# A 12-layer state-space block: GpSimd takes its ring products two tiles at a time

## The chip, the cores and the metric

The kernel runs on one core of a Trainium2 chip. TensorE multiplies matrices, VectorE and GpSimd work elementwise, ScalarE evaluates functions, SyncE (SP) issues loads. The metric is the device time of one launch in microseconds (us). A tile here is 128 partitions by 1024 float32 values unless a size is given.

## What is computed

Twelve layers over 8 sequences of 1024 tokens with 256 channels. In each layer the block is

```
xn = layernorm(x);  xp = xn @ pw.T + pb;  z = silu(xp)
for each direction (forward; backward on the reversed sequence):
    u = softplus(xp @ cw.T + cb)
    dt, B, C = split(u @ dbc_w.T)            # 32, 16, 16 columns
    delta = softplus(dt @ dtp_w.T + dtp_b)
    h_t = exp(delta_t * A) * h_(t-1) + (delta_t * u_t) * B_t      # for each of 16 states
    y_t = sum over the states of h_t * C_t  +  D * u_t
x = x + z * (y_forward + y_backward)
```

## The kernel before

The program walks through 96 steps, one per layer and batch element. A step has 64 tiles (`TILES`): 2 halves of the channels, 2 directions, 16 states. Tile k of a step is one recurrence over 1024 tokens for 128 channels. The backward direction's scan runs over the same tile in reverse.

Per tile these things happen, on different engines:

- ScalarE: `tile_exp` writes exp(delta * A) into one of 3 dA tiles (or, for the twelve `SHARED` tiles, into PSUM).
- TensorE: `rep_b` replicates row B of the state to 128 partitions in a PSUM tile `bv`; `add_up` adds the finished product into `y` in PSUM, five tiles behind.
- VectorE: `times_b` multiplies u by B in place (`bv`), `scan` does the recurrence into ring tile k % 8. The order is two `times_b`, then two scans, so tiles are scanned in pairs, and an even tile's scan is the first of its pair.
- GpSimd: `product` multiplies ring tile k % 8 by the replicated row C in `c` tile k % 4, in place. For the `SHARED` tiles, which have their B row loaded by DMA into `v`, GpSimd also does u * B (`times_b` on GpSimd, six tiles ahead).
- SP: `load_c` waits until the product of tile k - 4 is done and loads row C of tile k, broadcast to 128 partitions, 512 KB written per load; `load_b` loads `v`.

Beside this, each step prepares the next step's inputs (layer norm, projections, the softplus of both directions, delta and u). These operations are written into the slots of the 64 tiles by tables of slot numbers (`PROJ_AT`, `XS_AT` and so on): `prepare(k, ...)` issues on each engine what is due in slot k. On GpSimd that is: two normalisations (slots 5, 7, `w<-w,tmp`), two accumulating DMAs for the convolutions' softplus (`XS_AT`, slots 28 and 34), for each direction a subtraction `dbc<-dbc,parts` (`REST_AT` 41, 52) and one `parts<-dbc,parts` (`PARTS_AT` 43, 53), two accumulating DMAs of delta (`DELTA_AT` 43, 54) and the two products u = delta * xs of 128x2048 (`U_AT` 53, 58; the first is direction 1, the second direction 0). `finish`, in slot 5, adds the previous step's z into the output by an accumulating DMA. Each engine works its list strictly in order, so an operation in slot 58 stands behind all products up to 58. The next step's first `times_b` on VectorE waits for both u (`u_ready`).

An engine waits for another through a semaphore: `h_ready` counts finished scans, `p_ready` finished products, `c_loaded` landed C rows, one semaphore for each c tile.

Of the kernel before, what the change touches and what calls it, by code (L numbers as in the profile page):

```python
# [10 lines left out]
P = 128  # L11
# [6 lines left out]
def conv_seq_kernel(nc, x, ln_g, ln_b, proj_w, proj_b, convf_w, convf_b, convb_w, convb_b,  # L18
# [3 lines left out]
    T = HH * WW  # L22
# [7 lines left out]
    TILES = GROUPS * DT  # L30
# [5 lines left out]
    NDA, NR, NC, NV = 3, 8, 4, 2  # L36
# [4 lines left out]
    SHARED = (7, 11, 15, 21, 25, 29, 35, 39, 45, 49, 57, 61)  # L41
# [16 lines left out]
    PROJ_AT, XP_AT = (9, 11, 11, 15), (9, 10, 15, 19)  # L58
    CONV_AT = ((19, 21, 23, 25), (25, 25, 29, 31))
    CONV_OUT_AT = ((19, 23, 24, 24), (27, 27, 30, 30))  # L60
    XS_LOG_AT, XS_AT = ((24, 25), (31, 32)), (28, 34)
    DBC_AT, DBC_OUT_AT = ((32, 36), (41, 43)), ((35, 37), (44, 44))
    DTP_AT, DTP_OUT_AT = ((36, 37, 39, 39), (46, 49, 51, 52)), ((37, 38, 40, 40), (46, 51, 51, 51))
    HI_AT, REST_AT, MID_AT, PARTS_AT = (39, 44), (41, 52), (41, 54), (43, 53)
    DELTA_LOG_AT, DELTA_AT, U_AT = ((40, 40), (52, 55)), (43, 54), (53, 58)
    DIAG_AT, A_STEP_AT = 14, 14
    GATE_AT = 34
    LOADX_AT = 54
# [12 lines left out]
    with ExitStack() as ctx:  # L81
        def sb(name, shape, dt=F32):
            return ctx.enter_context(nc.sbuf_tensor(name, shape, dt))

        def sem(name):
            return ctx.enter_context(nc.semaphore(name))
# [34 lines left out]


        dA = [sb(f"dA{i}", [P, T]) for i in range(NDA)]
        ring = [sb(f"ring{i}", [P, T]) for i in range(NR)]
        c_sb = [sb(f"c{i}", [P, T]) for i in range(NC)]
        v_sb = [sb(f"v{i}", [P, T]) for i in range(NV)]
        assert len(SHARED) % NV == 0


        raw_w = sb("raw_w", [P, DT, D])  # L130
# [68 lines left out]
        h_ready = sem("h_ready")  # L199
        p_ready = sem("p_ready")  # L200
# [4 lines left out]
        c_loaded = [sem(f"c_loaded{i}") for i in range(NC)]  # L205
# [3 lines left out]
        def tiles(it, k):  # L209

            return it * TILES + (SEED + k)
# [32 lines left out]
        def early(it, n):  # L244

            return isinstance(it, int) and it < n
# [107 lines left out]
        def _(pool):  # L354
# [16 lines left out]
            pool.sem_inc(consts_ready, 1)  # L371
            pool.sem_inc(p_ready, SEED)

            def product(it, k, s):
                pool.wait_ge(h_ready, tiles(it, k + 1))
                pool.wait_ge(c_loaded[k % NC], it * (16 * TILES // NC) + (16 * (k // NC) + 16))
                nc.gpsimd.tensor_tensor(ring[k % NR][:], ring[k % NR][:], c_sb[k % NC][:],  # L377
                                        ALU.mult).then_inc(p_ready, 1)

            def times_b(it, k, s):  # L380
                c, d = k // HALF_TILES, (k // NS) % DIRS
                if k == SHARED[0]:
                    pool.wait_ge(u_ready, it * 2 + 2)
                i = SHARED.index(k)
                v = v_sb[i % NV][:]
                pool.wait_ge(vb_loaded[i % NV], it * (16 * len(SHARED) // NV) + 16 * (i // NV + 1))
                nc.gpsimd.tensor_tensor(v, u_of(d, s)[:, c, :], v, ALU.mult).then_inc(vp_ready, 1)  # L387
# [37 lines left out]
            def before_sums(k, n):  # L425

                for j in range(DIRS):
                    if k == XS_AT[j]:
                        pool.wait_ge(ln_done, n * CHAINS + (conv_chain[j] + 1))
                        pool.wait_ge(conv_out, n * (2 * FILLS) + (j + 1) * FILLS)  # L430
                    if k == DELTA_AT[j]:
                        pool.wait_ge(ln_done, n * CHAINS + (delta_chain[j] + 1))
                        pool.wait_ge(dtp_out, n * (2 * FILLS) + (j + 1) * FILLS)
# [8 lines left out]
            def finish(it, s, b):  # L442

                one = out_d[b] if isinstance(b, int) else out_d[bass.ds(b, 1)].rearrange("o p c t -> p (o c) t")
                pool.dma_start(one, z[s][:], accum_op=ALU.add).then_inc(stored, 16)

            def slots(it, s, k0, k1, more, weights, ended=None):
                for k in range(k0, k1):
                    if k == FIRST - 1 and not early(it, 1):
                        pool.wait_ge(gated, (it - 1) * DT + DT)  # L450
                    if more:
                        before_sums(k, it + 1)
                    product(it, k, s)
                    if k + V_AHEAD in SHARED:
                        times_b(it, k + V_AHEAD, s)
                    if k == FIRST - 1 and not early(it, 1):
                        finish(it - 1, 1 - s, ended)
                    if more:
                        prepare(k, it + 1, 1 - s)
                    if more > 1:  # L460
                        prepare(k - TILES, it + 2, s)
# [6 lines left out]
            def begin():  # L468
                pool.wait_ge(primed, 16 * NB)

            run_layers(nothing, slots, first_prepare, begin, tail, nothing, pool)


# [459 lines left out]
```

## Time and profile before

| | |
|---|---|
| median of 3 runs | 20557.72 us (20556.65 to 20569.37) |
| span of the profiled execution | 20567.5 us |
| VectorE, GpSimd, TensorE, ScalarE busy | 96%, 95%, 89%, 57% |
| granted TensorE clock | 0.9 or more of full speed in all 40 slices |
| DMA | 218 GB/s on the mean |
| products on GpSimd | 6144 of 128x1024 |
| a step on the mean, span / 96 | 214.2 us |

The span starts with the first and ends with the last instruction. Idle time of an engine counts only where something else waits for it; the views used below are the page's busy shares, the list of who waited for whom, and the timelines of two engines over the same stretch.

### The profile page before, as it was taken

How to read it: one execution, taken by the hardware profiler on the slowest of the kernel's cores; microseconds unless marked ns; L12 is line 12 of the kernel's file. 1: busy time of each engine (PE TensorE's matmuls, PEld its weight loads, DVE VectorE, ACT ScalarE, POOL GpSimd, SP SyncE). 2: the span in 40 equal slices, each digit the busy share in tenths (PEclk: the TensorE clock that was granted, in tenths of full speed). 3: DMA queues.
4: the chain of work that ended last, by engine and by line, in shares of the span. 5: the costliest groups of instructions: out<-in, count | busy, mean ns of one | idle time of the engine just before them, and what ended most of it. 6: DMA issues, size and time to landing. Idle time of an engine off the chain costs nothing.

```text
span 20567.5 us, 191522 instructions
## 1 busy us (share of the span) xinstructions
PE 18224.6 (89%) x45600; PEld 7539.9 (37%) x45600; DVE 19673.9 (96%) x11520; ACT 11649.3 (57%) x12409; POOL 19457.2 (95%) x8562
## 2 busy tenths in 40 slices
PE   8898888889888888888988888888888888889898
PEld 3333333333333333333333333333333333333333
DVE  7999999999999999999999999999999999999999
ACT  5555555555555555555655555555555555556554
POOL 7999999999999999999999999999999999999999
PEclk9999999999999999999999999999999999999999
DMA  6666666666666666666666666666666666667666
GB/s 203 217 220 217 222 220 217 220 219 223 218 218 223 215 221 218 218 220 218 222 217 222 220 218 223 215 219 217 218 222 216 222 219 219 218 220 223 217 220 202
DMA packets 1212383, 4489.98 MB, mean 218 GB/s; under 512 B 159872, under 2 KB 170624, under 8 KB 1161856
## 3 DMA queue, kind: packets, MB, share of 16 engines
q1 hardware_dynamic: 1078912, 3934.73, 54.7%
q0 software_dynamic: 81408, 503.35, 12.5%
q10 hardware_dynamic: 50688, 36.88, 0.9%
q8 instruction: 459, 7.52, 0.1%
q14 instruction: 916, 7.50, 0.1%
HBM read 3945.94 MB, written 134.22 MB: 198 GB/s over the span
## 4 chain that ended last, share of the span: by engine, by line
PE 33%; issue 28%; DVE 22%; ACT 7%; POOL 6%; DMA 3%; DVEq 1%; ACTq 0%; POOLq 0%; SPq 0%
PE y L719 19%; DVE ring L866 15%; DVE bv L850 6%; PE bank L738 6%; PE bv L709 5%; POOL ring L377 3%; DMA c<-c_rows 2%; ACT pre L555 2%; POOL u L422 1%; ACT bv L547 1%; PE y L731 1%; PE bank L785 1%; ACT dA L547 1%; ACT pre L559 1%; ACT tmp L555 1%
## 5 line engine op out<-in xcount | busy, mean ns | idle before, releaser
L377 POOL TENSOR_TENSOR ring<-ring,c 128x1024 f32<-128x1024 f32 x6144 | 14683.2, 2538 | 803.2 <-DVE ring L866 671.6
L719 PE MATMUL y<-ring,ident 128*128 128x512 f32 x24576 | 11737.2, 605 | 143.1 <-DVE z L872 140.5
L866 DVE TENSOR_TENSOR_SCAN ring<-dA,bv 128x1024 f32<-128x1024 f32 x4992 | 11192.3, 2274 | 192.0 <-ACT dA L547 39.5
L547 ACT ACTIVATE dA<-delta,a_step 128x1024 f32<-128x1024 f32 x4992 | 5608.6, 1143 | 3391.4 <-DVE ring L866 3126.0
L719 PEld LDWEIGHTS y<-ring,ident 128*128 128x128 f32 x24576 | 4745.5, 193 | 4506.3 <-issue 3663.7
L850 DVE TENSOR_TENSOR bv<-u,bv 128x1024 f32<-128x1024 f32 x4992 | 5924.3, 1214 | 437.7 <-PE bv L709 333.9
L709 PE MATMUL bv<-parts,select 128*128 128x512 bf16 x9984 | 3037.4, 386 | 2103.3 <-DVE ring L866 2081.3
L387 POOL TENSOR_TENSOR v<-u,v 128x1024 f32<-128x1024 f32 x1152 | 2907.2, 2524 | 0.0
L547 ACT ACTIVATE bv<-delta,a_step 128x1024 f32<-128x1024 f32 x1152 | 1286.4, 1117 | 2777.4 <-DVE ring L866 2777.3
L709 PEld LDWEIGHTS bv<-parts,select 128*128 128x128 bf16 x9984 | 671.2, 98 | 5707.1 <-DVE ring L866 5104.3
L866 DVE TENSOR_TENSOR_SCAN ring<-bv,v 128x1024 f32<-128x1024 f32 x1152 | 2608.5, 2264 | 2.3 <-POOL v L387 2.3
L738 PE MATMUL bank<-z,wt 128*128 128x512 f32 x3072 | 1413.5, 593 | 3.6 <-ACT xf L552 2.8
L551 ACT ACTIVATE tmp<-bank,vec 128x512 f32<-128x512 f32 x768 | 523.2, 681 | 889.7 <-PE bank L785 508.8
L551 ACT ACTIVATE pre<-bank,vec 128x512 f32<-128x512 f32 x768 | 522.6, 681 | 702.3 <-PE bank L738 658.1
L738 PEld LDWEIGHTS bank<-z,wt 128*128 128x128 f32 x3072 | 583.7, 190 | 740.5 <-issue 665.3
L785 PE MATMUL bank<-dbc,wt_dbc 128*128 128x512 f32 x1536 | 800.0, 614 | 8.4 <-ACT dbc L599 7.8
L738 PE MATMUL bank<-w,wt 128*128 128x512 f32 x1536 | 720.6, 602 | 46.1 <-POOL w L395 44.7
L738 PE MATMUL bank<-pre,mean_w 128*128 128x512 f32 x1536 | 714.6, 598 | 11.7 <-DMA pre<-in_x_dram 11.3
L395 POOL TENSOR_TENSOR w<-w,tmp 128x1024 f32<-128x1024 f32 x192 | 519.1, 2704 | 160.6 <-ACT tmp L649 160.6
L573 ACT ACTIVATE z<-bank,pbias 128x512 f32<-128x512 f32 x384 | 259.8, 677 | 595.0 <-PE bank L738 310.2
L552 ACT ACTIVATE delta<-bank,vec 128x512 f32<-128x512 f32 x768 | 522.3, 680 | 0.0
L404 POOL TENSOR_TENSOR dbc<-dbc,parts 96x1024 f32<-96x1024 f32 x192 | 409.7, 2134 | 76.4 <-PE bank L785 68.5
(66 smaller groups left out, 8904.8 us busy)
## 6 DMA issues: line engine op xcount, KB each, us to landing
c<-c_rows SPq DMA_DIRECT2D x6144, 512.0 KB, 4.6
v<-c_rows SPq DMA_DIRECT2D x1152, 512.0 KB, 5.0
w<-pre POOLq DMA_DIRECT2D x96, 1024.0 KB, 12.2
xf<-tmp POOLq DMA_DIRECT2D x96, 1024.0 KB, 10.9
delta<-pre POOLq DMA_DIRECT2D x96, 1024.0 KB, 8.4
delta<-tmp POOLq DMA_DIRECT2D x96, 1024.0 KB, 10.1
out_dram<-z POOLq DMA_DIRECT2D x96, 1024.0 KB, 13.2
pre<-out_dram SPq DMA_DIRECT2D x88, 1024.0 KB, 7.0
```

The costliest lines, as they stand in the source:

```text
L377: nc.gpsimd.tensor_tensor(ring[k % NR][:], ring[k % NR][:], c_sb[k % NC][:], ALU.mult).then_inc(p_ready, 1)
L387: nc.gpsimd.tensor_tensor(v, u_of(d, s)[:, c, :], v, ALU.mult).then_inc(vp_ready, 1)
L547: nc.scalar.activation(to[:], delta_of(d, s)[:, c, :], ACT.Exp, scale=a_step[s][:, c, n:n + 1]).then_inc(da_ready, 1)
L551: nc.scalar.activation(scratch[j][:, e, half(h)], bank[i % 2][:], ACT.Abs, bias=bias).then_inc(abs_done, 1)
L552: nc.scalar.activation(to[:, e, half(h)], bank[i % 2][:], ACT.Relu, bias=bias).then_inc(done, 1)
L555: nc.scalar.activation(scratch[j][:], scratch[j][:], ACT.Exp, scale=-1.0).then_inc(exp_done, 1)
L709: mm = pe.matmul(bv[k % 2][:, half(h)], select[:, n:n + 1].to_broadcast([P, P]), parts_of(d, s)[:, half(h)], start=True, stop=True)
L719: mm = pe.matmul(y[:, half(h)], ident[:], ring[k % NR][:, half(h)], start=(k % HALF_TILES == 0), stop=(k % HALF_TILES == HALF_TILES - 1), ...
L738: mm = pe.matmul(dst[:], lhs(c), rhs[:, c, half(h)], start=(c == 0), stop=(c == DT - 1))
L785: pe.matmul(bank[i % 2][:], wt_dbc[:, DT + e, :], dbc[:, half(h)], start=True, stop=True).then_inc(dtp_ready, 1)
L850: nc.vector.tensor_tensor(bv[k % 2][:], u_of(d, s)[:, c, :], bv[k % 2][:], ALU.mult).then_inc(v_ready, 1)
L866: nc.vector.tensor_tensor_scan(h, a, b, 0.0, ALU.mult, ALU.add).then_inc(h_ready, 1)
```

## The change

Ring and c tiles become slices of two tensors, `rings` (128 x 8 x 1024) and `c_rep` (128 x 4 x 1024), so that tiles k and k + 1 lie side by side. In each odd slot GpSimd multiplies the pair (k - 1, k) in one instruction of 128x2048. It waits for both scans and for both C rows, and raises `p_ready` by 2 when it is done. In even slots there is no product, and what else stands in an even slot follows directly on the slot before. Loads are issued as before, tile by tile, but since `p_ready` now moves in twos, the loads of a pair become due at the same moment. Three accumulating DMAs move by one slot: XS from (28, 34) to (27, 33), the second of delta from 54 to 55; the second u moves from slot 58 to 59.

```
-    XS_LOG_AT, XS_AT = ((24, 25), (31, 32)), (28, 34)
+    XS_LOG_AT, XS_AT = ((24, 25), (31, 32)), (27, 33)
-    DELTA_LOG_AT, DELTA_AT, U_AT = ((40, 40), (52, 55)), (43, 54), (53, 58)
+    DELTA_LOG_AT, DELTA_AT, U_AT = ((40, 40), (52, 55)), (43, 55), (53, 59)
...
-        ring = [sb(f"ring{i}", [P, T]) for i in range(NR)]
-        c_sb = [sb(f"c{i}", [P, T]) for i in range(NC)]
+        rings = sb("ring", [P, NR, T])
+        ring = [rings[:, i, :] for i in range(NR)]
+        c_rep = sb("c", [P, NC, T])
+        c_sb = [c_rep[:, i, :] for i in range(NC)]
...
-            def product(it, k, s):
-                pool.wait_ge(h_ready, tiles(it, k + 1))
-                pool.wait_ge(c_loaded[k % NC], it * (16 * TILES // NC) + (16 * (k // NC) + 16))
-                nc.gpsimd.tensor_tensor(ring[k % NR][:], ring[k % NR][:], c_sb[k % NC][:],
-                                        ALU.mult).then_inc(p_ready, 1)
+            def products(it, k, s):
+                pool.wait_ge(h_ready, tiles(it, k + 2))
+                for t in (k, k + 1):
+                    pool.wait_ge(c_loaded[t % NC], it * (16 * TILES // NC) + (16 * (t // NC) + 16))
+                two = rings[:, k % NR:k % NR + 2, :]
+                nc.gpsimd.tensor_tensor(two, two, c_rep[:, k % NC:k % NC + 2, :], ALU.mult).then_inc(p_ready, 2)
...
-                    product(it, k, s)
+                    if k % 2:
+                        products(it, k - 1, s)
```

Two places of GpSimd's order in a step. The first is around tiles 51 to 53: `v` is the multiply for tile 57 in slot 51, `dbc0` the rest, `u1_1` the u of direction 1. Before:

```order
L387 TENSOR_TENSOR v0<-u1_0,v0 128x1024
L375 REGISTER_ALU
L376 REGISTER_ALU
L377 TENSOR_TENSOR ring4<-ring4,c0 128x1024
L402 REGISTER_ALU
L404 TENSOR_TENSOR dbc<-dbc,parts0 96x1024
L375 REGISTER_ALU
L377 TENSOR_TENSOR ring5<-ring5,c1 128x1024
L416 ISA
L422 TENSOR_TENSOR u1_1<-delta1_1,w1 128x2048
```

After:

```order
L390 TENSOR_TENSOR v0<-u1_0,v0 128x1024
L405 REGISTER_ALU
L407 TENSOR_TENSOR dbc<-dbc,parts0 96x1024
L377 REGISTER_ALU
L379 REGISTER_ALU
L381 TENSOR_TENSOR ring<-ring,c 128x2048
L419 ISA
L425 TENSOR_TENSOR u1_1<-delta1_1,w1 128x2048
```

The rest now comes ahead of the product of tile 52, which it followed.

The second place is GpSimd from slot 55 to the u of direction 0 (`u0`). Before, it stands behind the product of tile 58 (ring tile 2), and the DMA of delta was issued ahead of these rows:

```order
L377 TENSOR_TENSOR ring7<-ring7,c3 128x1024
L387 TENSOR_TENSOR v1<-u1_0,v1 128x1024
L375 REGISTER_ALU
L376 REGISTER_ALU
L377 TENSOR_TENSOR ring0<-ring0,c0 128x1024
L375 REGISTER_ALU
L377 TENSOR_TENSOR ring1<-ring1,c1 128x1024
L375 REGISTER_ALU
L377 TENSOR_TENSOR ring2<-ring2,c2 128x1024
L420 ISA
L421 ISA
L422 TENSOR_TENSOR u0<-delta0,xf1 128x2048
```

After:

```order
L381 TENSOR_TENSOR ring<-ring,c 128x2048
L390 TENSOR_TENSOR v1<-u1_0,v1 128x1024
L417 DMA delta0<-tmp 128x2048
L377 REGISTER_ALU
L379 REGISTER_ALU
L381 TENSOR_TENSOR ring<-ring,c 128x2048
L377 REGISTER_ALU
L381 TENSOR_TENSOR ring<-ring,c 128x2048
L423 ISA
L424 ISA
L425 TENSOR_TENSOR u0<-delta0,xf1 128x2048
```

`u0` now stands behind the product of tile 59 too, and the DMA of delta behind the product of tile 55 and the multiply for tile 61.

## Rows read from the trace of the kernel before

**Rows 1.** The page: the span, and each engine's busy time (share), instructions.

```profile
span 20567.5 us, 191522 instructions
...
PE 18224.6 (89%) x45600; PEld 7539.9 (37%) x45600; DVE 19673.9 (96%) x11520; ACT 11649.3 (57%) x12409; POOL 19457.2 (95%) x8562
```

**Rows 2.** Waits, whole span: who waited for whom: us, times, longest.

```profile
POOL ring L377 <- DVE ring L866: 671.6, 394, 4.7
...
DVE bv L850 <- PE bv L709: 333.9, 445, 2.6
ACT z L573 <- DMA out_dram<-z: 284.9, 59, 6.1
...
DVE bv L850 <- POOL u L422: 12.9, 1, 12.9
```

**Rows 3.** VectorE's timeline, 11558 to 11656: start, us, line, operation, count, [idle before].

```profile
11560.69 4.46 DVE L866 TENSOR_TENSOR_SCAN ring<-dA,bv 128x1024 f32<-128x1024 f32 x2
...
11594.69 2.26 DVE L866 TENSOR_TENSOR_SCAN ring<-bv,v 128x1024 f32<-128x1024 f32 x1
...
11604.60 2.35 DVE L850 TENSOR_TENSOR bv<-u,bv 128x1024 f32<-128x1024 f32 x2
...
11647.40 4.46 DVE L866 TENSOR_TENSOR_SCAN ring<-dA,bv 128x1024 f32<-128x1024 f32 x2
```

**Rows 4.** GpSimd's timeline, 11563 to 11606, the same step.

```profile
11563.05 4.69 POOL L377 TENSOR_TENSOR ring<-ring,c 128x1024 f32<-128x1024 f32 x2 [0.18 <-DVE ring L866]
11567.68 2.36 POOL L387 TENSOR_TENSOR v<-u,v 128x1024 f32<-128x1024 f32 x1
11569.98 2.37 POOL L377 TENSOR_TENSOR ring<-ring,c 128x1024 f32<-128x1024 f32 x1
11573.04 2.13 POOL L404 TENSOR_TENSOR dbc<-dbc,parts 96x1024 f32<-96x1024 f32 x1 [0.69 <-PE bank L785]
11575.13 2.37 POOL L377 TENSOR_TENSOR ring<-ring,c 128x1024 f32<-128x1024 f32 x1
11577.45 4.54 POOL L422 TENSOR_TENSOR u<-delta,w 128x2048 f32<-128x2048 f32 x1
11581.97 2.12 POOL L409 TENSOR_TENSOR parts<-dbc,parts 32x1024 bf16<-32x1024 f32 x1
11584.07 2.36 POOL L377 TENSOR_TENSOR ring<-ring,c 128x1024 f32<-128x1024 f32 x1
11586.38 0.87 POOL L414 DMA_DIRECT2D delta<-tmp  x1
11586.99 2.65 POOL L377 TENSOR_TENSOR ring<-ring,c 128x1024 f32<-128x1024 f32 x1
11589.30 2.65 POOL L387 TENSOR_TENSOR v<-u,v 128x1024 f32<-128x1024 f32 x1
11591.61 7.28 POOL L377 TENSOR_TENSOR ring<-ring,c 128x1024 f32<-128x1024 f32 x3
11598.57 4.79 POOL L422 TENSOR_TENSOR u<-delta,xf 128x2048 f32<-128x2048 f32 x1
11603.05 4.94 POOL L377 TENSOR_TENSOR ring<-ring,c 128x1024 f32<-128x1024 f32 x2
```

**Rows 5.** The page's DMA issues: count, KB each, median us from issue to landing.

```profile
c<-c_rows SPq DMA_DIRECT2D x6144, 512.0 KB, 4.6
...
delta<-tmp POOLq DMA_DIRECT2D x96, 1024.0 KB, 10.1
```

**Rows 6.** Tile c, landings of two loads: from 8485.3 and 8485.8; from 11550.7 and 11553.0.

```profile
DMA to landing us min/median/max: 4.9/5.3/5.7
...
DMA to landing us min/median/max: 6.4/6.9/7.4
```

**Rows 7.** ScalarE's timeline, 11636 to 11656, the head of the next step.

```profile
11646.97 0.69 ACT L573 ACTIVATE z<-bank,pbias 128x512 f32<-128x512 f32 x1 [5.20 <-DMA out_dram<-z]
11647.56 1.14 ACT L547 ACTIVATE dA<-delta,a_step 128x1024 f32<-128x1024 f32 x1
```

More of the change, by code:

```diff
@@ L123, in conv_seq_kernel @@
         dA = [sb(f"dA{i}", [P, T]) for i in range(NDA)]
-        ring = [sb(f"ring{i}", [P, T]) for i in range(NR)]
-        c_sb = [sb(f"c{i}", [P, T]) for i in range(NC)]
+        rings = sb("ring", [P, NR, T])
+        ring = [rings[:, i, :] for i in range(NR)]
+        c_rep = sb("c", [P, NC, T])
+        c_sb = [c_rep[:, i, :] for i in range(NC)]
         v_sb = [sb(f"v{i}", [P, T]) for i in range(NV)]
-        assert len(SHARED) % NV == 0
+        assert len(SHARED) % NV == 0 and NR % 2 == 0 and NC % 2 == 0
         raw_w = sb("raw_w", [P, DT, D])
```

## The prediction

> **What bounds the kernel now.** I read the busy shares first. VectorE is busy 96% of the span, GpSimd 95%, TensorE 89% [rows 1]: an instruction saved on either of the first two could count, so the question is which of them waits for the other. The waits say it [rows 2]. GpSimd sat 671.6 us before its ring products because the scan on VectorE was not done, in 394 places. The other way round hardly anything stands: VectorE waited for GpSimd's u once (12.9 us), and its largest wait is for TensorE's replicated B rows, 333.9 us. So VectorE sets the pace, and GpSimd follows with some room. There are 96 steps, one per layer and batch element, of 20567.5 / 96 = 214.2 us on the mean; VectorE is idle (20567.5 - 19673.9) / 96 = 9.3 of them, GpSimd 11.6.
>
> The next reading is where GpSimd's room is smallest, since it also makes things VectorE needs at a fixed place. I took one usual step and set both engines' timelines side by side. Tile 51's scan ends at 11565.15 (two scans from 11560.69, 4.46 together) [rows 3]. Product 50 starts on GpSimd at 11563.05, as soon as scan 50 is done, and product 51 right behind it [rows 4]: here GpSimd waits for VectorE (0.18 us idle, released by the scan). From there to the end of the step GpSimd has more to do than VectorE: v for tile 57, one rest, u for direction 1, one parts, one DMA issue, v for tile 61, and then u for direction 0, which starts at 11598.57, takes 4.79 and ends at 11603.36 [rows 4]. The next step's first multiply by B on VectorE needs that u. It starts at 11604.60 [rows 3]. **The room is 1.24 us.** It was like that in nearly every step, since that wait is booked only once in 96 [rows 2]. This is the place on which the forecast rests: whatever makes u later by more than 1.24 us moves the whole of VectorE, once a step.
>
> **What the change removes.** 64 products of 128x1024 become 32 of 128x2048. What one costs is the distance from one start to the next: three products and the step into u take 11598.57 - 11591.61 = 6.96, so 2.32 each. The same engine already runs a two-input multiply of 128x2048, u: 11577.45 to 11581.97 is 4.52, 11598.57 to 11603.05 is 4.48 [rows 4]. I take 4.50 for a pair against 4.64, so 0.14 us less, 32 times a step: 4.5 us of GpSimd work a step. A row's own duration (2.36 for one) overlaps the next start and is not used for this. Most of this is room, not time, since GpSimd is not what is waited for; only the pairs between scan 51 and u are on the path. [...]
>
> **What it adds, one: the grain.** A pair starts when the second scan is done, not the first. Where GpSimd follows VectorE closely, product 50 started at 11563.05; the pair (50, 51) can start at 11565.2 at the earliest. And in the order after, u for direction 0 stands behind pair (58, 59) where it stood behind product 58; the DMA of delta also stands behind pair (54, 55) and v for 61, where it stood behind product 54.
>
> **The path from scan 51 to u, step by step**, with the durations of [rows 4]: pair (50, 51) from 11565.2, 4.50, to 11569.7. v for 57, 2.30, to 11572.0. The rest must wait for TensorE as before, until 11573.04 (the 0.69 idle before it), so 1.04 us of the delay is swallowed there; 2.09, to 11575.13. Pair (52, 53) to 11579.63. u of direction 1, 4.52, to 11584.15. parts, 2.10, to 11586.25. Pair (54, 55) to 11590.75. v for 61, 2.31, to 11593.06, whose recorded end is 11593.4; scan 61, which reads it, starts at 11594.69 [rows 3], so this is still in time. DMA issue 0.61, to 11593.67. Pairs (56, 57) and (58, 59) to 11602.67. u 4.79, to **11607.46**. That is 4.10 us later than 11603.36; less the room of 1.24, VectorE starts its next step **2.86 us later**.
>
> Two small things come on top. The accumulating transfer of delta, issued at 11593.06, takes 10.1 us to land [rows 5], so to 11603.2, and u cannot start at 11602.67: 0.5. And pair (50, 51) may be late itself, because of the loads below, by some 1.4; 1.04 of that is swallowed by the wait at the rest: 0.4. Together 3.75.
>
> **What it adds, two: the C loads.** There are four c tiles. A load was issued when the product four tiles back was done, with three products (6.9 us) to land in. Now the two loads of a pair go out together when the pair two back is done, and have one pair, 4.50 us, plus whatever small work lies between. A lone load lands after 4.6 [rows 5]. Of loads issued behind one another the last is later: two of them 0.48 us apart behind a v load landed after 4.9 and 5.7 [rows 6], so the second 6.2 after the first was issued; without the v load I take 5.5 (0.45 + 5.05, an estimate between the lone load's 4.6 and that 5.7). Where nothing lies between two pairs, that is a wait of 1.0 us. Six of the 32 places are so bare (in front of the pairs that begin at tiles 0, 14, 28, 38, 48 and 50; at 28 only a DMA issue lies between), the others have a v multiply or more (2.3 us) and are covered. Where an accumulating transfer runs beside them loads took 6.4 to 7.4 [rows 6], so in front of pair (48, 49), behind the first delta transfer, I expect 2 to 3 us. Between tiles 26 and 50 these waits cost GpSimd only room: it waits for scans there anyway. In front of u, pairs (52, 53) to (58, 59) have 7 us or more to land in, so nothing is on the path but the 0.4 above. [...]
>
> **What it adds, three: the head of a step.** Behind u, four products (9.3) become two pairs (9.0), but VectorE starts right after u instead of 1.24 later, and pair (0, 1) waits 1.0 for its loads. So against VectorE GpSimd is 1.2 + 1.0 - 0.3 = 1.9, later 1.6 us behind where it was. What hangs on it: the output transfer, for whose landing ScalarE waits 5.20 us before it writes z at 11646.97 [rows 7]. The exp of tile 13 stands behind that, 11647.56 to 11648.70; scan 13 is the second of the two from 11647.40, so about 11649.6 [rows 3]: room 0.9. A delay of 1.6 leaves 0.7 of stall, in the steps that have the wait (59 of 96 [rows 2]), so 0.4 a step. TensorE's sums read the products five tiles later; they are hardly ever waited for, and I charge nothing.
>
> **The sum.** 3.75 + 0.4 = 4.1 us a step on VectorE's chain, at 95 boundaries: 390 us. The profiled span is 20567.5 [rows 1] and the median 20557.7, so the difference is applied to the median: **20950 us**, 1.9% slower. XS issued one slot earlier (27, 33) goes out about as early as before against VectorE; it costs nothing.
>
> **Rivals.** (1) *GpSimd paces, and its saving is what counts*: then 32 x 0.14 = 4.5 us a step off, less the waits for C of bare places in the stretch where it is behind (2 x 1.0), so 2.5 x 96 = 240 us: 20320. It decides if the waits of VectorE for TensorE (333.9) were at bottom waits for a product. Against it: GpSimd waited for scans, 671.6. (2) *No change*: u is not later by more than its room. It needs 2.9 us that I do not see, for instance pairs that take 4.1 instead of 4.50; and the rest of the program the same. 20520 to 20600. (3) *The C loads reach the path to u*. Pair (58, 59) has v for 61, the DMA issue and one pair before it, 2.31 + 0.61 + 4.50 = 7.4 us for its two loads, and the delta transfer starts among them. If loads there land as beside the other transfer, 7.4, plus 0.45 for the later issue and 0.8 for standing behind the first (5.7 - 4.9) [rows 6], the second is there after 8.7, so 1.3 late; and the same in front of (48, 49) and (50, 51) lets the chain start 3 us late instead of 1.4, 1.5 more. That is 2.8 a step on top of 4.1, 95 x 6.9 = 655 us: 21210. It decides from landings of 7.4 us in front of (58, 59). The other bare places do not reach VectorE as long as GpSimd's sum, 202.7 - 4.5 of work and some 5 to 12 of waits for loads, stays under the step. (4) That the pair would be split back into two instructions is ruled out by the compiled order.
>
> **How the numbers follow.** The forecast (u late, 2.9 to 5 us a step, 20780 to 21050) 0.70; the C loads, 21100 to 21350, 0.17; faster 0.08; no change 0.05. A measurement of this kernel tells 0.2% (41 us) from nothing. Slower holds 0.87. The range reaches from the forecast's bottom, 95 x 2.86 = 272 us with some room below it, to the middle of rival 3: 20780 to 21260; some 0.2 is left out.
>
> **What would show it.** Right: u on VectorE's list of waits (its multiply by B waiting for GpSimd's u, some 3.5 us, in nearly all steps); GpSimd's product group near 4.5 us each, 3072 of them; more idle time of GpSimd for c landings, in front of pairs 0, 14 and 48 above all, and less for scans; ScalarE's wait for the output transfer longer. Wrong: if that wait for u stays single, or VectorE's new idle time stands before scans, or before multiplies released by TensorE that itself waited for products, the grain acted elsewhere. If c landings are waited for in front of (58, 59), rival 3 has it.

## The result

The changed kernel takes 21365.07 us (median of 4 runs, 21349.62 to 21379.4) against 20557.63 us: the ratio is 1.0389, 95% interval 1.0377 to 1.0402. Slower was forecast and came, but twice as much of it: 8.4 us a step instead of 4.1, and the time lies outside the range. The profiled execution spans 21347.5 us, 780 us more than before.

The page of the changed kernel, first the span and busy times as in [rows 1], then the two groups of GpSimd and VectorE that carry the change: line, engine, operation, shapes, count | busy, mean ns | idle before, releaser.

```profile
span 21347.5 us, 185442 instructions
...
PE 18395.0 (86%) x45600; PEld 7562.9 (35%) x45600; DVE 19697.5 (92%) x11520; ACT 11641.0 (55%) x12409; POOL 19048.5 (89%) x5490
...
L381 POOL TENSOR_TENSOR ring<-ring,c 128x2048 f32<-128x2048 f32 x3072 | 14090.0, 4632 | 2044.9 <-DMA c<-c_rows 956.8
...
L870 DVE TENSOR_TENSOR_SCAN ring<-bv,v 128x1024 f32<-128x1024 f32 x1152 | 2611.5, 2267 | 359.8 <-ACT bv L551 351.2
```

GpSimd has 409 us less to do and VectorE's work is nearly unchanged (19697.5 against 19673.9, 24 us more), so 756 of the 780 us are idle time of VectorE, and the question is what it waits for. Its list of waits, to be held against [rows 2]:

```profile
DVE bv L854 <- PE bv L713: 368.3, 439, 5.5
DVE ring L870 <- ACT bv L551: 351.2, 93, 5.6
DVE bv L854 <- POOL u L425: 350.1, 96, 12.3
DVE z L876 <- PE y L723: 153.8, 192, 8.5
DVE bv L854 <- issue: 125.0, 34, 5.6
```

Two rows have grown from next to nothing, and both now come once in nearly every step. The wait for u is the one that the prediction rests on: 12.9 us, once, has become 350.1 us, 96 times. The other stands before the scan of a tile whose exp ScalarE writes into `bv`, 351.2 us in 93 places; the prediction does not know it. Together they are 688 of the 780 us more.

**The wait for u.** GpSimd's timeline and then VectorE's at the end of a step (scan 51 ends here at 12018.65), to be held against [rows 3, 4].

```profile
12016.46 9.03 POOL L381 TENSOR_TENSOR ring<-ring,c 128x2048 f32<-128x2048 f32 x2 [2.68 <-DMA c<-c_rows]
12025.44 2.35 POOL L390 TENSOR_TENSOR v<-u,v 128x1024 f32<-128x1024 f32 x1
12027.76 2.12 POOL L407 TENSOR_TENSOR dbc<-dbc,parts 96x1024 f32<-96x1024 f32 x1
12029.85 4.54 POOL L381 TENSOR_TENSOR ring<-ring,c 128x2048 f32<-128x2048 f32 x1
12034.35 4.55 POOL L425 TENSOR_TENSOR u<-delta,w 128x2048 f32<-128x2048 f32 x1
...
12057.35 4.70 POOL L425 TENSOR_TENSOR u<-delta,xf 128x2048 f32<-128x2048 f32 x1
```

```profile
12057.36 1.20 DVE L884 TENSOR_TENSOR w<-pre,bank 128x1024 f32<-128x1024 f32 x1
12062.18 2.36 DVE L854 TENSOR_TENSOR bv<-u,bv 128x1024 f32<-128x1024 f32 x2 [3.62 <-POOL u L425]
```

Pairs (48, 49) and (50, 51) follow each other from 12016.46, so (50, 51) starts about 12020.97, 2.3 us behind scan 51. u ends at 12062.05 (12057.35 + 4.70), 43.4 us behind the end of scan 51; before it was 38.2 (11603.36 - 11565.15), so 5.2 more. VectorE waits 3.62 us.

**The wait at scan 45.** ScalarE's timeline of the changed kernel around it, then VectorE's.

```profile
11988.14 1.13 ACT L551 ACTIVATE dA<-delta,a_step 128x1024 f32<-128x1024 f32 x1
11995.12 1.04 ACT L624 CAST parts<-dbc 64x1024 bf16<-64x1024 f32 x1 [5.84 <-POOL dbc L407]
11996.07 1.11 ACT L551 ACTIVATE bv<-delta,a_step 128x1024 f32<-128x1024 f32 x1
```

```profile
11991.05 2.29 DVE L870 TENSOR_TENSOR_SCAN ring<-dA,bv 128x1024 f32<-128x1024 f32 x1
11997.30 2.29 DVE L870 TENSOR_TENSOR_SCAN ring<-bv,v 128x1024 f32<-128x1024 f32 x1 [3.96 <-ACT bv L551]
```

The exp of tile 45 stands on ScalarE behind a cast, and the cast waits 5.84 us for GpSimd's rest (the subtraction `dbc<-dbc,parts` in slot 41). Before, the same three pieces stood like this (ScalarE, before; the rest started on GpSimd at 11536.35):

```profile
11538.46 1.13 ACT L547 ACTIVATE dA<-delta,a_step 128x1024 f32<-128x1024 f32 x1
11539.50 1.03 ACT L620 CAST parts<-dbc 64x1024 bf16<-64x1024 f32 x1
11540.44 1.11 ACT L547 ACTIVATE bv<-delta,a_step 128x1024 f32<-128x1024 f32 x1
```

No wait at all. Taken from the scan of tile 44 (11541.37 before, 11991.05 after), the rest has gone from 5.0 us ahead of it to 1.9 us behind it. Why it is 6.9 us late is in GpSimd's timeline of the changed kernel, tiles 26 to 41:

```profile
11940.30 4.55 POOL L381 TENSOR_TENSOR ring<-ring,c 128x2048 f32<-128x2048 f32 x1 [4.65 <-ACT pre L563]
11944.77 0.90 POOL L415 DMA_DIRECT2D w<-pre  x1
...
11954.19 4.55 POOL L381 TENSOR_TENSOR ring<-ring,c 128x2048 f32<-128x2048 f32 x1 [1.66 <-DMA c<-c_rows]
11961.88 4.54 POOL L381 TENSOR_TENSOR ring<-ring,c 128x2048 f32<-128x2048 f32 x1 [3.13 <-ACT tmp L563]
...
11968.67 0.85 POOL L415 DMA_DIRECT2D xf<-tmp  x1
...
11981.65 4.54 POOL L381 TENSOR_TENSOR ring<-ring,c 128x2048 f32<-128x2048 f32 x1 [3.05 <-DMA c<-c_rows]
...
11992.94 2.14 POOL L407 TENSOR_TENSOR dbc<-dbc,parts 96x1024 f32<-96x1024 f32 x1
```

Pair (26, 27) is held 4.65 us and pair (32, 33) 3.13 us, by ScalarE's Ln (the logarithm of the softplus): in an odd slot the wait that belongs to the accumulating transfer (`before_sums`) is written ahead of the pair, and since the slots moved from 28 and 34 to 27 and 33 it holds the pair up. The second transfer then goes out at 11968.67, 10.5 us behind the start of scan 34, where it was 6.0 before, and runs beside the C loads for (38, 39). These were issued from 11974.1, 6.1 and 7.0 us to landing, and the pair stands 3.05 us for them:

```profile
L308 SPq DMA_DIRECT2D c<-c_rows x2: 320/680/1040, 11974.1 to 11974.5; - x2
...
DMA to landing us min/median/max: 6.1/6.5/7.0
```

### The profile page after: what moved, and what is told of

Same layout as the page of the kernel before. It is cut to its first block, busy times and chain, and to the rows that moved or that the text cites. A ratio compares the mean times of both kernels' runs of the same rounds, so it can differ in the third digit from the quotient of the medians.

```text
span 21347.5 us, 185442 instructions
## 1 busy us (share of the span) xinstructions
PE 18395.0 (86%) x45600; PEld 7562.9 (35%) x45600; DVE 19697.5 (92%) x11520; ACT 11641.0 (55%) x12409; POOL 19048.5 (89%) x5490
## 4 chain that ended last, share of the span: by engine, by line
issue 25%; PE 21%; POOL 20%; DMA 14%; DVE 14%; ACT 4%; SPq 1%; DVEq 1%; POOLq 0%; ACTq 0%
DMA c<-c_rows 14%; POOL ring L381 14%; PE y L723 12%; DVE ring L870 10%; PE bank L742 5%; DVE bv L854 4%; PE bv L713 3%; POOL u L425 2%; POOL dbc L407 1%; POOL v L390 1%; POOL parts L412 1%; ACT pre L563 1%; ACT pre L559 1%; PE y L735 1%; SPq L308 1%
## 5 line engine op out<-in xcount | busy, mean ns | idle before, releaser
L381 POOL TENSOR_TENSOR ring<-ring,c 128x2048 f32<-128x2048 f32 x3072 | 14090.0, 4632 | 2044.9 <-DMA c<-c_rows 956.8
L723 PE MATMUL y<-ring,ident 128*128 128x512 f32 x24576 | 11864.0, 610 | 331.2 <-POOL ring L381 188.4
L854 DVE TENSOR_TENSOR bv<-u,bv 128x1024 f32<-128x1024 f32 x4992 | 5932.3, 1214 | 859.1 <-PE bv L713 368.3
L713 PE MATMUL bv<-parts,select 128*128 128x512 bf16 x9984 | 3108.4, 394 | 2528.0 <-DVE ring L870 2507.6
L870 DVE TENSOR_TENSOR_SCAN ring<-bv,v 128x1024 f32<-128x1024 f32 x1152 | 2611.5, 2267 | 359.8 <-ACT bv L551 351.2
L390 POOL TENSOR_TENSOR v<-u,v 128x1024 f32<-128x1024 f32 x1152 | 2771.5, 2406 | 0.0
L624 ACT CAST parts<-dbc 64x1024 bf16<-64x1024 f32 x192 | 199.0, 1037 | 535.2 <-POOL dbc L407 535.2
```

Of the source, the lines that this page charges most:

```text
L381: nc.gpsimd.tensor_tensor(two, two, c_rep[:, k % NC:k % NC + 2, :], ALU.mult).then_inc(p_ready, 2)
L713: mm = pe.matmul(bv[k % 2][:, half(h)], select[:, n:n + 1].to_broadcast([P, P]), parts_of(d, s)[:, half(h)], start=True, stop=True)
L723: mm = pe.matmul(y[:, half(h)], ident[:], ring[k % NR][:, half(h)], start=(k % HALF_TILES == 0), stop=(k % HALF_TILES == HALF_TILES - 1), ...
L854: nc.vector.tensor_tensor(bv[k % 2][:], u_of(d, s)[:, c, :], bv[k % 2][:], ALU.mult).then_inc(v_ready, 1)
L870: nc.vector.tensor_tensor_scan(h, a, b, 0.0, ALU.mult, ALU.add).then_inc(h_ready, 1)
```

## The experiments

There were three theories. **A**: two waits of VectorE a step make the loss, for u and at scan 45, fed by the grain of two and by the slots. **B**: the C landings pace everything. **C**: the moved slots alone do it. In the code below, "..." marks lines left out. Ratios are to the kernel before, measured in the same rounds.

**The slots alone.** The kernel before with only the new slot numbers.

```
-    XS_LOG_AT, XS_AT = ((24, 25), (31, 32)), (28, 34)
+    XS_LOG_AT, XS_AT = ((24, 25), (31, 32)), (27, 33)
...
-    DELTA_LOG_AT, DELTA_AT, U_AT = ((40, 40), (52, 55)), (43, 54), (53, 58)
+    DELTA_LOG_AT, DELTA_AT, U_AT = ((40, 40), (52, 55)), (43, 55), (53, 59)
```

> The kernel before with single products, but with the new slot numbers (XS 27 and 33, second DELTA 55, second U 59). Theory A (two waits of VectorE a step make the whole loss: for u at the head of a step, and at scan 45 for ScalarE's exp, which stands behind a cast that waits for GpSimd's rest; both fed by the grain of pairs): the slots alone cost u one product, 2.3 us less the room of 1.24, so about 1.1 us a step and no wait at scan 45, since GpSimd still has its idle 4 us in front of tile 38 to absorb the waits for the Ln: 20660, ratio 1.005. Theory B (waits for C landings set the time): nothing, 1.000. Theory C (the slot moves do it, because GpSimd waits for ScalarE's Ln ahead of tiles 27 and 33): most of the loss, 1.02 or more, with the wait at scan 45 in its waits.

Measured 20842.88 us, ratio 1.0135 (1.0118 to 1.0152). VectorE's waits:

```profile
DVE bv L850 <- PE bv L709: 365.4, 468, 2.4
DVE z L872 <- PE y L719: 257.8, 192, 7.9
DVE bv L850 <- POOL u L422: 163.8, 94, 12.8
...
DVE ring L866 <- ACT bv L547: 1.7, 6, 0.5
```

The wait for u is there (163.8 us; without the 12.8 that the first step has in the kernel before too, 1.6 a step, expected 1.1) and nothing at scan 45, as A says: GpSimd waits 390.3 and 241.9 us for the Ln, and its waits for scans fall by about as much, from 671.6 to 33.7, so single products absorb it. But the loss is more than twice the 0.5% that I expected. The rest is mostly in the second row: z waits 257.8 us. Before:

```profile
DVE z L872 <- PE y L719: 158.9, 192, 7.9
```

This wait is not a later product 63: it ends 49.5 us behind scan 51 in a step of either kernel, since u has only changed places with product 59. z waits for TensorE's last sums, and these are slower. In one step each, the four matmuls ahead of z at the head of a step are

```profile
11624.01 1.88 PE L719 MATMUL y<-ring,ident 128*128 128x512 f32 x4
```

```profile
11791.41 3.51 PE L719 MATMUL y<-ring,ident 128*128 128x512 f32 x4
```

The first row is of the kernel before, the second of this run. The granted clock is 1.00 over the first and 0.53 over the second, which is nearly all at the lower of TensorE's two levels, 1.2 of 2.4 GHz. z waits 0.31 us there and 2.01 here. Over the whole trace these last sums ran at a granted clock under 0.75 at the head of 68 of 96 steps, against 8 before, and z's wait at the head is 137.6 us, against 47.4. TensorE had waited 3.30 us for a scan at 11775.47, and the clock over its next 3.4 us of sums was 0.50; but a wait of 2.12 us stands just ahead of the last sums in both kernels. So what brings the clock down there is not shown; that the late u does it, by holding up the scans that TensorE waits for, was not tested. C falls: the slots alone are 1.35% of 3.9%.

**The grain without the long instruction.**

```
-two = rings[:, k % NR:k % NR + 2, :]
-nc.gpsimd.tensor_tensor(two, two, c_rep[:, k % NC:k % NC + 2, :], ALU.mult).then_inc(p_ready, 2)
+nc.gpsimd.tensor_tensor(ring[k % NR], ring[k % NR], c_sb[k % NC], ALU.mult)
+nc.gpsimd.tensor_tensor(ring[k % NR + 1], ring[k % NR + 1], c_sb[k % NC + 1], ALU.mult).then_inc(p_ready, 2)
```

> The changed kernel with the same waits, the same signals by twos and the same slots, but two instructions of 128x1024 instead of one of 128x2048. Theory A: the loss is the grain's and the slots', not the instruction's; two take 4.64 instead of 4.50, five pairs stand on the way to u and about three on the way to the rest, so 1.1 us a step more than the changed kernel: 21470, ratio to before 1.044. If the long instruction itself did harm, it would come out faster than the changed kernel, under 21300.

Measured 21491.75 us, ratio 1.0455 (1.0437 to 1.0472), as A forecast. Against two short instructions the long one is a gain of 127 us, 1.3 a step, where it stands on the way to what VectorE waits for. The loss is not the instruction's: it comes with the waits and signals of the pair, and with the slots, which are the changed ones here too.

**XS behind the pair.** A 128x1 multiply carries the wait in the even slot.

```
-    XS_LOG_AT, XS_AT = ((24, 25), (31, 32)), (27, 33)
+    XS_LOG_AT, XS_AT = ((24, 25), (31, 32)), (28, 34)
...
+elif more and k in (*XS_AT, *DELTA_AT):
+    q = (*XS_AT, *DELTA_AT).index(k)
+    one = mark[:, q:q + 1]
+    nc.gpsimd.tensor_tensor(one, one, one, ALU.mult)
```

> The changed kernel with XS back in slots 28 and 34, where GpSimd has no product: the wait for ScalarE's Ln and the accumulating transfer then stand behind pairs (26, 27) and (32, 33), not around them (a 128x1 multiply of GpSimd carries the wait). Theory A and C: GpSimd's 4.2 and 2.4 us of waiting for the Ln run beside the pairs, the second transfer goes out some 5 us earlier, the loads of (38, 39) land before they are needed, the rest is early enough and the wait at scan 45 (3.6 us a step) goes; the wait for u (3.4) stays: 21365 - 96 x 3.6 = 21020, ratio 1.022. Theory B: under 1 us a step, 1.035 or more.

Measured 20958.87 us, ratio 1.0194 (1.0177 to 1.0211). Half of the loss is gone, and with it the wait at scan 45; the one for u stays. VectorE's waits (the row for ScalarE's `bv` has 4.5 us left):

```profile
DVE bv L858 <- PE bv L717: 374.9, 448, 7.2
DVE bv L858 <- POOL u L425: 308.3, 96, 12.4
DVE z L880 <- PE y L727: 175.2, 192, 8.5
```

**u early, XS as changed.** Second DELTA back to 54, second u back to 58, where it stands behind pair (56, 57); the same 128x1 multiply.

```
-    DELTA_LOG_AT, DELTA_AT, U_AT = ((40, 40), (52, 55)), (43, 55), (53, 59)
+    DELTA_LOG_AT, DELTA_AT, U_AT = ((40, 40), (52, 55)), (43, 54), (53, 58)
```

> The changed kernel (XS stays at 27 and 33) with only the second DELTA back in slot 54 and the second u in 58, so u stands behind pair (56, 57). Theory A: the wait for u (3.4 us a step) goes, the one at scan 45 (3.6) stays, and with e4 and e5 the two parts add up: 21365 - 96 x 3.3 = 21050, ratio 1.024. If the two waits hide each other, it stays above 1.032.

Measured 21099.48 us, ratio 1.0255 (1.0238 to 1.0272). The mirror image: u is back at one wait, scan 45 keeps its own.

```profile
DVE bv L858 <- PE bv L717: 469.2, 555, 7.0
DVE ring L874 <- ACT bv L555: 346.0, 91, 4.9
...
DVE bv L858 <- POOL u L425: 12.7, 1, 12.7
```

It gives 2.8 us a step back, against the 3.3 forecast and u's wait of 3.5 (337.4 / 96); part of it turns up as waits for TensorE's B rows (469.2 against 368.3).

**All old slots, pairs kept.**

```
-    XS_LOG_AT, XS_AT = ((24, 25), (31, 32)), (27, 33)
+    XS_LOG_AT, XS_AT = ((24, 25), (31, 32)), (28, 34)
...
-    DELTA_LOG_AT, DELTA_AT, U_AT = ((40, 40), (52, 55)), (43, 55), (53, 59)
+    DELTA_LOG_AT, DELTA_AT, U_AT = ((40, 40), (52, 55)), (43, 54), (53, 58)
```

> The changed kernel with all the old slot numbers (XS 28 and 34, second DELTA 54, second U 58), so the pairs alone: u then stands behind pair (56, 57), one pair earlier than in the changed kernel. Theory A: the wait for u goes as well (4.5 us earlier against 3.4), what stays is some 1 us at the head of a step: 20650, ratio 1.005 (1.00 to 1.01). Theory B: the C landings still set it, 1.03. If the grain alone is the cause and the slots do not matter: 1.03 or more.

The 128x1 multiply is in this run too. Measured 20753.61 us, ratio 1.0093 (1.0076 to 1.0110), inside the range that A forecast. Both waits are gone, and three quarters of the loss. B falls as the whole cause: GpSimd still stands 731.5 us for C landings, not much less than the 956.8 of the changed kernel, at a quarter of the loss. GpSimd's largest waits here:

```profile
POOL ring L381 <- DMA c<-c_rows: 731.5, 516, 4.8
POOL ring L381 <- DVE ring L874: 712.9, 398, 4.3
```

What is left of the loss, 195 us, is in two rows of VectorE: waits for B rows, 462.3 us against 333.9 before, and for z, 231.5 against 158.9. TensorE's loads of the sums' weights wait 517.0 us for pairs on GpSimd, against 126.4 for products before, and the last sums at the head of a step ran at a granted clock under 0.75 in 59 of 96 steps, against 8.

The four corners can now be put side by side: the slots alone cost 1.35%, the pairs alone 0.93%, both together 3.89%. So 1.6%, some 330 us, needs both at once.

**The cast behind the exp.** In the changed kernel ScalarE casts one slot later.

```
-HI_AT, REST_AT, MID_AT, PARTS_AT = (39, 44), (41, 52), (41, 54), (43, 53)
+HI_AT, REST_AT, MID_AT, PARTS_AT = (39, 44), (41, 52), (42, 54), (43, 53)
```

> The changed kernel with ScalarE's cast of the rest one slot later (MID 42 for 41), so that the exp of tile 45 stands ahead of it and no longer behind GpSimd's rest. The cast itself is ready at the same time as before, since it waits for the rest anyway. Theory A: the wait of scan 45 goes though GpSimd is as late as ever, the wait for u stays: 21020, ratio 1.022. Theory B (the C landings pace everything through GpSimd): no change, 1.039, the wait turns up elsewhere.

Measured 21358.33 us, ratio 1.0380 (1.0363 to 1.0398): nothing gained beyond the intervals, and my expectation under A was wrong. The wait moved:

```profile
DVE bv L854 <- PE bv L713: 402.2, 447, 4.7
DVE ring L870 <- ACT dA L551: 382.0, 104, 5.3
DVE bv L854 <- POOL u L425: 336.5, 96, 12.6
```

Now a scan with a dA tile waits, 382.0 us in 104 places instead of `bv`'s 351.2 in 93. By position it is tile 48 (95 of the 104), whose exp stands on ScalarE behind the copies of dbc, which wait for GpSimd's `parts` (550.1 us, against 452.3 in the changed kernel), the next thing behind rest and cast. The cast, one slot later, still waits for the rest (365.0 us, 95 times). So the cause is not that one exp stands behind one cast. It is that the run of GpSimd's rest, ScalarE's cast and GpSimd's parts is late as a whole, and ScalarE meets it in two places. Letting ScalarE pass the first only makes it wait at the second.

**Half the bytes of the C loads, changed kernel.** The second half of the columns of c is zero, so half of the tokens get no sum over the states.

```
-sp.dma_start(c_sb[k % NC][:], c_rows[s, d, NS + n:NS + n + 1, :].to_broadcast([P, T])
+sp.dma_start(c_sb[k % NC][:, 0:HALF], c_rows[s, d, NS + n:NS + n + 1, 0:HALF].to_broadcast([P, HALF])
...
```

> The changed kernel whose C loads bring only the first 512 of 1024 columns (the other half of each c tile is zero, so half of the tokens get no sum over the states): the same number of loads with half the bytes. Theory A: bare places lose their 1.0 us wait, those at 38 and 48 (3.1 and 2.2 a step) fall to about 1; the rest comes some 2 us earlier and scan 45 waits 1.3 instead of 3.6, u 2.6 instead of 3.4: 21050, 1.024. Theory B: the whole loss goes, under 1.01.

Measured 20942.48 us, ratio 1.0180 (1.0163 to 1.0197), some 100 us below the forecast of A. GpSimd's wait for C falls from 956.8 to 221.3, scan 45's from 351.2 to 72.3, u's from 350.1 to 279.0.

```profile
DVE bv L855 <- POOL u L426: 279.0, 96, 10.8
...
DVE ring L871 <- ACT bv L552: 72.3, 52, 3.3
```

The wait at scan 45 needs both: a GpSimd made late by the Ln, and C loads that land late. Taking away either one, here or by XS, removes most of it. Nearly half of the loss stays, so B is not the whole cause; but the landings are worth over half of it in the changed slots.

**Half the bytes, old slots.** The same edit on the pairs in their old slots.

> The pairs in the old slots (as e5_old_slots) with C loads of 512 columns, so that half of the tokens get no sum over the states. It parts what is left of the loss (0.9%, at the head of a step: z waiting for the last sum, B rows waiting behind a sum) into loads and grain. If the waits for landings in front of pairs (62, 63) and (0, 1), 0.9 and 1.0 a step, make it: 20600, ratio 1.002. If the grain (a sum of an even tile cannot start before its pair is done, 2.3 us later) makes it: 20720, 1.008.

Measured 20688.8 us, ratio 1.0059 (1.0042 to 1.0076), between the two forecasts: of the 0.9% that pairs cost in the old slots, 0.3 goes with the landings and 0.6 stays with nearly no landing waited for (121.8 us).

**Pairs in a part of the step.** Single products for the tiles outside, with the old slots and the 128x1 multiply (in the first of the two, u of direction 0 in slot 57). The second has 16 and 40 for the 8 and 56 below.

```
-if k % 2:
+if not 8 <= k < 56:
+    product(it, k, s)
+elif k % 2:
     products(it, k - 1, s)
...
```

> Pairs only for tiles 8 to 55, single products for tiles 56 to 63 and 0 to 7, XS 28 and 34, DELTA 43 and 54, u of direction 0 in slot 57 (behind product 57). If what is left of the loss in the old slots (0.9%, and 0.6% with half loads) is the grain at the head of a step, where the last sums, z and the first B rows stand behind products, it goes: 20570, ratio 1.0005 (0.999 to 1.003). If it is the grain elsewhere or the C landings in the middle: it stays at 1.006 to 1.009.

> Pairs only for tiles 16 to 39, where GpSimd waits for scans anyway, single products elsewhere, old slots (XS 28 and 34, DELTA 43 and 54, u in 58). GpSimd saves 12 x 0.14 us a step and nothing waits for it there: 20560, ratio 1.000, neither gain nor loss. A ratio under 0.998 would say that GpSimd's work itself counts; one over 1.003 that the grain costs in the middle of a step too.

Pairs for 8 to 55: 20650.06 us, ratio 1.0042 (1.0028 to 1.0056). Pairs for 16 to 39: 20601.68 us, ratio 1.0013 (1.0004 to 1.0022). The first was expected at 1.0005 and is a miss: the head of the step is about half of what was left, not all of it. What remains is spread over small waits, most of it for TensorE's B rows, 383.3 us here against 333.9, and its cause stays open. The second was expected at 1.000 and comes close, with an interval just above it: GpSimd's saved work gains nothing there either. The fewer pairs, the nearer to the kernel before, and never under it: no version beat it.

## Why the prediction was wrong

**The bound and the direction** were right: VectorE paces, GpSimd's saved work does not make the kernel faster, and rival 1 did not happen. The pair costs what was taken, 4.50 from start to start (12029.85 to 12034.35).

**The term for u** was right in place and size: 3.75 us a step expected, 350.1 / 96 = 3.65 measured. Its inside was less good. The delta transfer was to hold u for 0.5; it landed in 7.9 us instead of 10.1 and did not. The chain was to start 1.4 late; it started 2.3 late, since the wait for C in front of (48, 49) came as said (2.68, expected 2 to 3), but on a GpSimd already held. The two misses offset each other, so that the sum came out this close is in part luck.

**The step that failed** is in the paragraph on the C loads: "Between tiles 26 and 50 these waits cost GpSimd only room: it waits for scans there anyway." It does wait for scans there, but something on the way to VectorE's scans waits for it. In slot 41 stands the rest, ScalarE's cast waits for it, and exps stand behind the cast and behind the copy that needs `parts`. I had looked for GpSimd's smallest room at one exit (u) and taken the list of waits as proof that there was no other. The full list of waits before, of which [rows 2] has a part, did show one: ScalarE waits for `parts` in nearly every step. The row before, then the one that has joined it in the changed kernel:

```profile
ACT dbc L599 <- POOL parts L409: 374.4, 94, 5.0
```

```profile
ACT parts L624 <- POOL dbc L407: 535.2, 96, 7.5
```

The first cost VectorE nothing, and I did not ask how far ScalarE's wait could grow. What the prediction put at nothing became 351.2 us of VectorE's time at scan 45, 3.66 a step. Both ways of taking it away gave it back: XS moved back (4.5 us left) and half the bytes of the C loads (72.3 left).

**The second error** is one sentence: "XS issued one slot earlier (27, 33) goes out about as early as before against VectorE; it costs nothing." The wait for the Ln is written ahead of the product in that slot, so moving the transfer to an odd slot moves a wait in front of a pair: 417.0 and 235.2 us of GpSimd's time. Moved back, it gave 4.2 us a step. Nor does the transfer go out as early as before: the second one goes out 4.5 us later against the scans (10.5 us behind the start of scan 34 for 6.0).

**The head of a step** was miscounted. "Behind u, four products (9.3) become two pairs (9.0)": before, five products stood behind u (59 to 63, 11.6 us), since u was behind product 58. With five, GpSimd is not 1.9 us later against VectorE but 0.4 earlier (1.2 + 1.0 - 2.6), and the term of 0.4 a step has nothing to stand on; the wait that was to carry it fell, 253.6 from 284.9. What grew at the head is something else: z's wait there, 90.3 us from 47.4, with the last sums at a granted clock under 0.75 in 32 of 96 steps for 8, which a smaller wait of z in the middle of the step makes up for (63.5 from 111.6), and VectorE's idle time put down to "issue", 125.0 from 73.8. "TensorE's sums ... are hardly ever waited for, and I charge nothing" was also too easy: TensorE waits 188.4 us for pairs before its sums (2.5 for products before). In the changed kernel VectorE's waits for B rows grew by only 34 us, but with the pairs in the old slots by 128.

**The rivals**: 3 named the right agent, C landings late beside a transfer, at the wrong place ((58, 59), where no landing was waited for). Its 21210 is too low as well. The range was built around one exit of GpSimd and so could not hold a second one of the same size.

The sum as it was: u 3.65 - 0.13, scan 45 3.66, B rows 0.36, issue 0.53, together 8.1 of the 780 / 96 = 8.1 us a step; smaller rows cancel.

## What to carry to other kernels

Before merging two instructions on an engine, list every engine that reads anything it makes, and at each exit look for the room, not only for the wait: an engine with no waiter on the critical one can still have a waiter that has a waiter. What counts is not the work of the merged instruction but when its inputs must all be there and when its outputs are handed on; saving 0.14 us a pair can cost up to 2.3 us, one product, at each end of a chain. When an operation is moved by a slot, read which waits are written with it and what stands behind them in the new place.

## What the runs showed of the hardware

Two loads of 512 KB issued together do not fit behind one pair of 4.5 us. At a bare place (tile 0) GpSimd waited 0.79 us; beside an accumulating transfer, loads issued 0.4 us apart took 6.1 and 7.0 us and cost 3.05. The row for tile 0, changed kernel:

```profile
12071.78 4.53 POOL L381 TENSOR_TENSOR ring<-ring,c 128x2048 f32<-128x2048 f32 x1 [0.79 <-DMA c<-c_rows]
```

The accumulating transfer of delta, 1024 KB issued by GpSimd, took 10.1 us to land in the kernel before and 7.9 in the changed one (medians of 96). The Trainium skill (DMA: Bandwidth & Descriptors, Anatomy of one DMA — SWDGE (gpsimd) path) fits 2.0 us and size over 436 GB/s to a transfer that GpSimd issues, which makes 4.4 us for this one, an estimate. The trace disagrees.

The same group of four matmuls of TensorE's sums took 1.88 us at a granted clock of 1.00 and 3.51 us at 0.53. In the run of the slots alone the slow case came at the head of 68 of 96 steps, and what it cost shows as a wait of VectorE for z.
